# Turning order and PSUM banks in the second and third step of a round, and the place of two small copies on ScalarE, in a fused attention and feed-forward kernel

## What is computed

```python
def reference(x, ctx, hops, ...):
    q, k, v = layernorm(x), ctx, ctx                    # 8 heads of 64
    ig, fg = gates(concat(q, k, v))                     # per head and token
    log_f  = log_sigmoid(fg)
    log_D  = cumsum(log_f)[:, None] - cumsum(log_f)[None, :] + ig   # causal
    m      = max(log_D, -1);  D = exp(log_D - m)
    C      = (q @ k.T / 8 + einsum("vc,vmc->vm", q, rpe[hops])) * D
    h      = C / (max(|sum(C)|, exp(-m)) + 1e-6) @ v
    x      = x + layernorm_per_head(h) * (1 + ln_w) + ln_b
    y      = layernorm(x)
    p      = softmax(y @ gate_w.T);  two best of 10, null experts dropped, renormalised
    return x + y @ base_w.T + base_b + 2 * sum_e w_e * (y @ lora_A[e].T) @ lora_B[e].T
```

## Time and profile before

| what | value |
|---|---|
| time, median of 3 runs | 3451.86 us (3441.05 to 3455.0) |
| span of the profiled execution | 3448.0 us |
| its time outside the span, by the median | 3.9 us |
| pipeline of rounds, from the first gates matmul at 1608.7 us on, one round | about 62.8 us |
| PE busy, of the whole span | 3024.2 us (88%) |
| DVE / POOL / ACT busy, of the whole span | 72% / 59% / 56% |
| granted clock of PE in the rounds | 1.00, of 2.4 GHz |

### The profile page before, as it was taken

One profiled execution on the slowest core, in us unless ns is written; L12 is line 12 of the kernel. 1 busy time (PEld: TensorE's weight loads), 2 busy tenths in 40 slices (PEclk: granted clock), 3 DMA queues, 4 the chain that ended last, 5 costly groups with the idle time before them and its releaser, 6 DMA issues.

```text
span 3448.0 us, 69897 instructions
## 1 busy us (share of the span) xinstructions
PE 3024.2 (88%) x24660; PEld 1878.3 (54%) x24660; DVE 2480.0 (72%) x5141; ACT 1914.6 (56%) x4581; POOL 2023.7 (59%) x2195
## 2 busy tenths in 40 slices
PE   3777877777778777799999999999999999999997
PEld 2445555454445444455655556556655665566554
DVE  3555555555555555688888888888888888888875
ACT  0444444444444444466666666666666666666663
POOL 3777777777777776255454454554554545545454
PEclk7898888999999999899999999999999999999999
DMA  4999999999999999655555555555555555555542
GB/s 111 322 350 347 326 344 350 341 348 350 347 348 346 347 349 322 190 170 172 172 180 169 162 182 167 172 178 174 174 169 166 182 170 170 178 174 177 171 139 67
DMA packets 412814, 799.46 MB, mean 232 GB/s; under 512 B 107034, under 2 KB 211482, under 8 KB 410420
## 3 DMA queue, kind: packets, MB, share of 16 engines
q1 hardware_dynamic: 311476, 453.08, 42.1%
q0 software_dynamic: 82560, 270.60, 23.5%
q10 hardware_dynamic: 18432, 71.31, 5.3%
HBM read 618.02 MB, written 176.69 MB: 230 GB/s over the span
## 4 chain that ended last, share of the span: by engine, by line
PE 58%; DMA 14%; POOL 11%; issue 6%; DVE 5%; SPq 3%; ACT 3%; POOLq 0%; ACTq 0%; DVEq 0%
DMA arena<-in_L_xattn_rpe_dram,arena 14%; PE psum L1684 11%; PE psum L1605 8%; PE psum L1635 7%; PE psum L1617 7%; POOL arena L749 6%; PE psum L1522 6%; PE psum L1549 5%; PE psum L1538 4%; PE psum L1664 3%; PE psum L1688 3%; PE psum L1580 2%; SPq L585 2%; POOL arena L740 2%; PE psum L1491 1%
## 5 line engine op out<-in xcount | busy, mean ns | idle before, releaser
L749 POOL DMA_INDIRECT arena<-in_L_xattn_rpe_dram,arena x768 | 730.3, 951 | 234.0 <-issue 183.4
L1522 PE MATMUL psum<-arena 128*128 128x128 f32 x4128 | 620.9, 299 | 217.7 <-DMA arena<-in_L_xattn_rpe_dram,arena 203.1
L1522 PEld LDWEIGHTS psum<-arena 128*128 128x128 f32 x4128 | 493.7, 152 | 454.0 <-DMA arena<-in_L_xattn_rpe_dram,arena 317.1
L932 ACT ACTIVATE arena<-arena 128x512 f32<-128x512 f32 (+3 forms) x1024 | 496.8, 555 | 42.8 <-PE psum L1635 39.2
L1684 PE MATMUL psum<-arena 128*128 128x512 f32 x1024 | 494.7, 597 | 3.7 <-DVE arena L1324 1.8
L1274 DVE TENSOR_TENSOR arena<-psum,arena 128x1024 f32<-128x1024 f32 (+1 forms) x384 | 387.1, 1043 | 150.4 <-PE psum L1617 141.1
L543 DVE COPY arena<-psum 128x512 f32<-128x512 f32 x384 | 263.5, 689 | 244.1 <-PE psum L1522 237.9
L552 DVE COPY arena<-psum 128x416 f32<-128x416 f32 (+15 forms) x512 | 225.1, 442 | 288.7 <-PE psum L1538 276.8
L1538 PE MATMUL psum<-arena 64*32 64x416 f32 (+7 forms) x8192 | 368.1, 426 | 59.1 <-ACT arena L854 39.4
L768 POOL TENSOR_SCALAR_AFFINE_SELECT arena<-arena 128x256 f32<-128x256 f32 x256 | 129.0, 504 | 491.2 <-ACT arena L932 490.2
L543 ACT COPY arena<-psum 128x512 f32<-128x512 f32 x384 | 225.8, 588 | 283.6 <-PE psum L1522 279.8
(11 more groups left out here) (110 smaller groups left out, 4725.9 us busy)
## 6 DMA issues: line engine op xcount, KB each, us to landing
arena<-in_x_dram SPq DMA_DIRECT2D x256, 256.0 KB, 4.3
arena<-gate_rows SPq DMA_DIRECT2D x128, 512.0 KB, 4.4
arena<-in_x_dram SPq DMA_DIRECT2D x512, 64.0 KB
arena<-in_ctx_dram SPq DMA_DIRECT2D x32, 1024.0 KB, 7.4
out_dram<-arena SPq DMA_DIRECT2D x128, 256.0 KB, 2.1
arena<-in_L_xattn_rpe_dram,arena POOLq DMA_INDIRECT x1032
arena<-hop_products SPq DMA_DIRECT2D x128, 128.0 KB, 2.6
arena<-hop_products SPq DMA_DIRECT2D x128, 120.0 KB, 2.6
```

Of the source, the lines that this page charges most:

```text
L749: nc.gpsimd.indirect_dma_start(out=rows[set_of(n, v)][:, t, :], out_offset=None, in_=rpe[:, :], in_offset=bass.IndirectOffsetOnAxis(ap=her ...
L932: last = nc.scalar.activation(decay[u % DECAYS][:, e, at:at + width], top_pair[p % 2][:, e * S + j * P:e * S + j * P + width], ACT.Exp, bi ...
L1522: last = nc.tensor.transpose(turn_bank(o)[:, q * P:(q + 1) * P], own[:, q * P:(q + 1) * P], ident)
```

## The change

1. In the second step the turned tiles use three banks. Context tile 3 is turned first (bank 7), then context tile 2, now into bank 5, then query tile 0 (bank 6) and query tile 1 (bank 7). ACT copies context tile 3 ahead of tile 2. Query tile 0 no longer waits for a copy of a context tile; the turn into bank 5 waits for DVE's sum of the pair that used it (`("sum", 3)` of `rf`), and the weighing of unit 3, which writes bank 5, now waits for the copy of context tile 2.
2. In the third step feed-forward tile 0 is turned second, ahead of the first pair's `turn_back`.
3. On ACT, `mix_turned(rf, 0)` stands ahead of the logarithm of `gate_log` (now a function of its own, `gate_softplus`), and `mix_turned(rf, 1)` ahead of `unit_decay(ra, 10)`.

No instruction is added or removed, and the lists of DVE, POOL and SP are the same as before.

```diff
-        C_TURN, C_BANK = [0, 0, 1, 1], [4, 7, 6, 7]
+        C_TURN, C_BANK = [0, 0, 1, 1], [4, 7, 5, 7]
...
-                      [("c", 0), ("c", 1), ("ln", 2), ("rstd", 2), ("c", 2), ("c", 3), ("x", 0), ("x", 1),
+                      [("c", 0), ("c", 1), ("ln", 2), ("rstd", 2), ("c", 3), ("c", 2), ("x", 0), ("x", 1),
...
+                def gate_softplus():
                     act.wait_ge(act_p.sem, act_p.done(rp.b, "exp"))
...
+                    keys(3)
                     keys(2)
-                    keys(3)
...
                 if rf:
                     mix_turned(rf, 0)
+                if rp:
+                    gate_softplus()
...
+                if rf:
+                    mix_turned(rf, 1)
                 if ra:
                     unit_decay(ra, 10)
                 if rf:
-                    mix_turned(rf, 1)
                     ffn_turned(rf, 2)
...
                     elif t == 2:
+                        if rf:
+                            pe.wait_ge(dve_o.sem, dve_o.done(rf.b, ("sum", 3)))
+                    else:
+                        pe.wait_ge(act_p.sem, act_p.done(rp.b, ("c", 1)))
...
+                def turn_queries(t):
+                    pe.wait_ge(dve_p.sem, dve_p.done(rp.b, ("norm", t)))
+                    if t == 0:
                         pe.wait_ge(act_p.sem, act_p.done(rp.b, "stats", 1))
                         if rg:
                             pe.wait_ge(*dve_f.at(rg.b, ("out", ST - 1)))
                     else:
-                    pe.wait_ge(act_p.sem, act_p.done(rp.b, (("c", 2), ("c", 3), ("x", 0), ("x", 2))[t]))
+                        pe.wait_ge(act_p.sem, act_p.done(rp.b, (("c", 3), ("x", 0), ("x", 2))[t - 1]))
...
+                    if u == 3 and rp:
+                        pe.wait_ge(act_p.sem, act_p.done(rp.b, ("c", 2)))
...
                     if rp and d == 1:
+                        turn_context(3)
                         turn_context(2)
-                        turn_context(3)
...
+                    if rf and d == 2:
+                        turn_ffn(rf, 0)
                     if ra and d in BACK:
                         turn_back(ra, BACK[d])
-                    if d == 2:
-                        if rf:
-                            turn_ffn(rf, 0)
-                        if rp:
-                            turn_queries(3)
+                    if rp and d == 2:
+                        turn_queries(3)
```

More of the change, by code:

```diff
@@ L396, in build @@
                       ["zi", "abs", "min", "logf", "cum", "a", "cmax", "maxlog"])
-        pe_p = Stage(sem("pe_p"), [("c", t) for t in tiles] + [("x", t) for t in tiles] + ["gates", "stats"])
+        pe_p = Stage(sem("pe_p"), [("c", t) for t in (0, 1, 3, 2)] + [("x", t) for t in tiles] + ["gates", "stats"])
         act_p = Stage(sem("act_p"), [(n, t) for t in (0, 1) for n in ("ln", "rstd")] +
-                      [("c", 0), ("c", 1), ("ln", 2), ("rstd", 2), ("c", 2), ("c", 3), ("x", 0), ("x", 1),
+                      [("c", 0), ("c", 1), ("ln", 2), ("rstd", 2), ("c", 3), ("c", 2), ("x", 0), ("x", 1),
                        ("ln", 3), ("rstd", 3), ("x", 2), ("x", 3), "gctx", "exp", "ln", "floor", "stats"])
@@ L1561, in turn_context @@
                     elif t == 2:
-                        pe.wait_ge(act_p.sem, act_p.done(rp.b, "stats", 1))
-                        if rg:
-                            pe.wait_ge(*dve_f.at(rg.b, ("out", ST - 1)))
+                        if rf:
+                            pe.wait_ge(dve_o.sem, dve_o.done(rf.b, ("sum", 3)))
                     else:
@@ L1570, in turn_queries @@
                     pe.wait_ge(dve_p.sem, dve_p.done(rp.b, ("norm", t)))
-                    pe.wait_ge(act_p.sem, act_p.done(rp.b, (("c", 2), ("c", 3), ("x", 0), ("x", 2))[t]))
+                    if t == 0:
+                        pe.wait_ge(act_p.sem, act_p.done(rp.b, "stats", 1))
+                        if rg:
+                            pe.wait_ge(*dve_f.at(rg.b, ("out", ST - 1)))
+                    else:
+                        pe.wait_ge(act_p.sem, act_p.done(rp.b, (("c", 3), ("x", 0), ("x", 2))[t - 1]))
                     turn(X_BANK[t], xq_norm[t % 2]).then_inc(pe_p.sem, pe_p.step(("x", t)))
```

## The result

The changed kernel took 3430.28 us (median of four runs, 3424.1 to 3431.83), the kernel before, run beside it, 3453.43 (3441.05 to 3458.53): a ratio of 0.9936 with a 95% interval of 0.9914 to 0.9957. It is 0.64% faster; the forecast was 3428, with a range of 3414 to 3445.

A forecast was written before the change was run, and what follows sets the result against it. PE was taken as the bound, so only its waits could be won: rounds of 61.74 plus 0.25 us for late mixes, 61.99 against 62.78, 0.79 us in 30 rounds, 24 us, giving 3428 us from 3451.86; range 3414 to 3445.

The forecast's parts named there:

- Second step: Context and query turns on PE: with a third bank only the fourth tile waits, 0.44 us won a round.
- Third step: Turns up to `routes` on PE: `routes` starts 0.67 us sooner in sum, 0.23 of it from turning feed-forward tile 0 second.
- Fourth step: PE's `base(rf, 0)` waits for DVE's sum, which was to end 7.12 us after the old round start instead of 7.83.
- Shared in proportion: Other view of the DVE and POOL port: no saving on line 1229, round 0.27 us longer than by the lock.
- rival 1: DVE's sum hangs on POOL's weighted tiles and doesn't move: at most 0.3 us a round, 9 us, 3443 us; chance 0.21.
- the short round's sum: DVE's sum in the short 62.18 us round, 7.12 us after its start, taken as the upper end of the gain.
- Fifth step: PE from the turned mix to tile 2's turn: the 0.29 us wait for ACT's copy goes, leaving 0.97 us.
- The logarithm: ACT's copy of tile 0's mix ahead of the gates' logarithm: taken as 0, at most 0.08 us a round.
- The long rounds: PE's wait for tile 1's late mix, behind a late tile of x: 0.25 us a round added.
- The sum: All terms together: rounds of 61.99 against 62.78 us, 0.79 us less, 24 us over 30 rounds.
- rival 2: Fifth step bound by a later mix of tile 1, wait growing in every round: slower, 3472 us; chance 0.05.
- Rival 3: All of PE's waits go, DVE's chain out of the way: 1.45 us a round, 43 us, 3408 us; chance 0.07.

The follow-up runs named there:

- e1: The changed kernel with the second step's old two banks and tile order back, the other two parts kept; 3439.54 us, 0.9961 of the kernel before.
- e4: The changed kernel without the router's guard operation on DVE, a constant 1e-30 in the sum instead; 3403.86 us, 0.9855 of the kernel before.
- e7: The changed kernel, guard kept, with POOL weighting tile 1 ahead of adding tile 0's bias; 3421.35 us, 0.9912 of the kernel before.
- e3: The changed kernel with the copy of tile 1's mix behind unit 10's exponentials again; 3433.30 us, 0.9943 of the kernel before.
- e9: The changed kernel with the gates' logarithm ahead of the copy of tile 0's mix again; 3423.7 us, one run.

## Why the prediction was right, point by point

*Second step: right.* 0.50 - 0.06 = 0.44 was forecast, and from the first turn to the weighing 2.43 - 1.94 = 0.49 came. The fourth tile waits 0.08 where 0.06 was forecast. The 0.05 more come from the kernel before, whose fourth tile stood too, for 0.05 us (its first instruction at 2040.18, 0.13 after the one ahead of it), which the forecast didn't count. Neither new wait shows.

*Third step: right.* From the second step's first turn to `routes` it was 8.89 us and is now 8.11, 0.78 sooner, where 0.67 was forecast: 0.49 for 0.44, and 2.15 - 1.86 = 0.29 for 0.23.

*Fourth step: the number right, its reason half.* The forecast had the sum end 7.12 us after the old round's start. It ends 2736.07 - 2728.15 = 7.92 after a start that lies 0.81 earlier, thus at 7.11. `base` waits 0.36 instead of 0.23, as PE is 0.1 earlier than thought.

Two reasons were given. One, that the operation on line 1229 (1234 now) would no longer meet a POOL instruction at its start, holds: it took 1.07 to 1.10 us in 18 of 27 rounds before and takes no more than 0.58 us in the 100 instances between 1733.7 and 3286 us after, and e1 shows that the lost race costs 0.7 us of a round. The Trainium skill (SBUF — State Buffer, Who interferes with whom) states that whoever issues first gets the shared port pair for the whole instruction and that the other is blocked. The rows agree as far as the wait goes: the 1.08 us end with POOL's instruction. Shared in proportion, the sum would have ended at 7.83 - 0.44 = 7.39.

The other reason, that DVE's chain would follow the scores by 0.44, doesn't hold. In the kernel before, the rounds that win the race have the sum at 7.12 too, with scores that come 0.49 later. What holds it there is POOL, whose weighting of tile 1 has not moved, and two more meetings with POOL (1374 beside 797, 1360 beside 776): e4 takes the second away, e7 the first, and each ends the wait. That is the mechanism of rival 1 inside the forecast's number. The prediction took "the short round's sum" as "already POOL's and DVE's best shown", a bound read off a round without saying what set it; the number came out right because POOL's order of work sets the same bound before and after. That was in part luck, and e4 and e7 show that it was no floor.

*Fifth step: right.* 0.97 us from the turned mix to the turn, as written, and undoing it costs 0.29 (e3).

*The logarithm: right,* at 0 in a usual round and 0.06 on average (e9).

*The long rounds: the size right, the cause incomplete.* 0.25 us a round was added for the late mix of tile 1. The mean lies 62.08 - 61.81 = 0.27 above the usual round, and 0.22 of that are the six rounds with this wait. The prediction put it down to a late tile of x alone. In the long round of the windows above, DVE, POOL and PE read:

```profile
1804.81 1.27 POOL L781 TENSOR_TENSOR arena<-arena 128x512 f32<-128x512 f32 x1 [2.60 <-DMA arena<-in_x_dram]
1808.46 0.87 DVE L1374 TENSOR_TENSOR arena<-arena 128x512 f32<-128x512 f32 x1 [1.56 <-POOL arena L791]
1815.22 1.26 POOL L781 TENSOR_TENSOR arena<-arena 128x512 f32<-128x512 f32 x1
1815.22 1.27 DVE L1360 SCALAR_TENSOR_TENSOR arena<-arena 128x1 f32<-128x1 f32 x1
1817.14 0.33 PE L1659 MATMUL psum<-arena 128*128 128x128 f32 x1 [0.96 <-DVE arena L1365]
```

The tile is late, as in the earlier trace rows, and 1.56 us of it reach DVE. But then the guard of tile 1 waits out a whole POOL instruction that starts with it, 1.27 us for 0.16, and PE stands 0.96. In exactly the six rounds between 62.4 and 63.2 that guard takes 1.00 to 1.28 us; in the other 21 it takes 0.16. How late the layer is does not decide it: line 1374 starts 12.72 us after the round's start in the round from 2107.64, which has no such wait, and 12.35 after it in the one from 2294.46, which has. Without the guard (e4) DVE still waits up to 2.8 us for POOL at the layer, and no wait of PE for the mix is shown. Starts tell more: in the three rounds of e4 that take 62.0 to 62.2, PE turns that mix 20.35 to 20.49 us after the round's start, where a usual round of e4 turns it at 20.04, and the gates' columns behind it (line 1599) lose 0.3 more. So a late layer (12.97 to 13.12 us after the round's start there) still costs up to 0.45 us of the mix's time.

*The sum.* 0.79 us a round and 24 us were forecast; 62.80 - 62.09 = 0.71 a round, 22.4 us in the pipeline and 23 in the time came. The forecast round was 61.99 us, from 62.78, which is 0.02 too little. Of the 0.10 by which the round is longer than forecast, 0.07 is the usual round (61.81 for 61.74) and the rest lies in the others.

*The rivals.* Rival 1's end (rounds near 62.5, 3443) did not come, though its mechanism is there; rival 2's wait occurs in 6 of 24 rounds and not in most. Rival 3's time, 3408, is reached in e4 (3404), not by this change alone but with one operation of DVE less.

## What to carry to other kernels

When PE's waits are ended by small copies, compute after each gain what is late next: here the 0.3 us won in the third step stay hidden behind another engine's chain until that is shortened, and are worth 9 us then. A bound that was read off a good round should be followed back to what sets it: here POOL's order of work did, and moving it by one place was worth 0.4 us a round. A chain of short DVE operations beside a busy POOL should be read by the largest duration of each line, not by its mean: a line that shows 0.16 as its median and 1.28 as its largest meets POOL, and removing it, or moving POOL's work by one place, can be worth about as much as a rearranged engine list. And where a race gives rounds two lengths, count both in the profile before a median of few runs is believed: the six executions of e1 lay up to 12 us apart.

## What the hardware showed that was not expected

Which of DVE's operations are held by POOL follows their operands. The view by line and shape in the kernel after, all instances: shortest / median / longest in ns, first and last start.

```profile
L1360 DVE SCALAR_TENSOR_TENSOR arena<-arena x128: 158/159/1283, 1491.7 to 3422.4; 128x1 f32<-128x1 f32 x128
L1374 DVE TENSOR_TENSOR arena<-arena x128: 670/868/1510, 1476.7 to 3412.9; 128x512 f32<-128x512 f32 x128
L1355 DVE SCALAR_TENSOR_TENSOR arena<-arena,psum x128: 223/224/226, 1491.2 to 3422.0; 128x8 f32<-128x8 f32 x128
L1358 DVE TENSOR_REDUCE arena<-arena x128: 160/161/163, 1491.5 to 3422.2; 128x1 f32<-128x8 f32 x128
L1234 DVE TENSOR_SCALAR arena<-arena x128: 173/379/817, 1396.3 to 3289.9; 128x8 f32<-128x8 f32 x128
```

The first two have two inputs in SBUF, and whenever one began with 0.1 us or more of a POOL instruction still to run it was held: 34 times on line 1360 (687 to 1004 ns), 90 times on line 1374 (848 ns and more, 670 to 694 otherwise). The one with an input in PSUM (1355) began so 93 times, the reduction (1358) 63 times and the reciprocal (1362) 32 times, and none of them took longer than its other instances. The Trainium skill (SBUF — State Buffer, Who interferes with whom) says of a VectorE instruction with two SBUF inputs that it contends with a GpSimd instruction that reads SBUF. This trace agrees.

Line 1234 has a single tile as input and is held too, in all 63 such instances (375 to 817 ns). Line 1352, which is the same kind of operation but writes to PSUM, began so 94 times and always took 287 to 292 ns. The Trainium skill (SBUF — State Buffer, Who interferes with whom) counts operations of this kind among those that can take the shared pair in a two-port mode; no run here shows the mode.

The size was the surprise: one element per partition can wait 1.1 us. And the lock is decided by differences that the trace can't show. In e1 the recorded start of line 1234 lies 3 to 24 ns ahead of POOL's wherever the two meet, and the operation took 0.17 us in some cases and 1.08 in others, both at the same 20 ns. Finally, a held operation can overlap its wait by a part of its own time: line 1374's addition ended at 2728.97 + 1.51 = 2730.48, 0.55 after the first POOL instruction on line 797 ended (2729.93), and alone it takes 0.67. The second one on that line took 1.49 us there, the first 1.04.
